# u x D accumulated by TensorE in the turned sums, gate and GLU read from PSUM, seven of 32 products on GpSimd, in a fused selective-scan layer

## The reference

```python
x  = x + attn(rotate_and_decay(x, condB_deltat))      # residual 1
x  = x + ffn(lora_mlp(x, expert_ids))                 # residual 2

def attn(x):
    xn  = layer_norm(x) * ln_g + ln_b
    x_f = mamba(xn)
    x_r = flip(mamba(flip(xn, 1)), 1)
    y   = gelu(concat([x_f, x_r]) @ dim_reduce_w.T + dim_reduce_b)
    g   = y @ glu_w.T + glu_b
    return g[..., :H] * sigmoid(g[..., H:]) + x

def mamba(x):
    xi, z = split(x @ in_proj_w.T)                    # 256 channels each
    u     = silu(causal_conv4(xi) + conv_b)
    dt, B, C = split(u @ x_proj_w.T)                  # 64, 16, 16
    delta = softplus(dt @ dt_proj_w.T + dt_proj_b)
    h_t   = exp(delta_t * A) * h_(t-1) + delta_t * u_t * B_t   # 16 states a channel
    y_t   = sum over the 16 states of h_t * C_t
    return ((y + u * D) * silu(z)) @ out_proj_w.T

def lora_mlp(x, e):   # relu MLP 128 -> 512 -> 128, weights merged with expert e's LoRA
def ffn(x):           # (silu(w1 x) * (w2 x)), gelu(h1 .), gelu(h2 .), w3
```

## Time and profile before

| | before |
|---|---|
| median of 3 runs | 1112.46 us (1112.07 to 1113.34) |
| the profiled execution's own time | 1109.67 us |
| its span, first to last instruction | 1107.5 us |
| mean granted TensorE clock | 0.937 |
| PE busy | 926.2 us, 84% |
| DVE busy | 921.2 us, 83% |
| POOL busy | 874.9 us, 79% |
| ACT busy | 775.3 us, 70% |
| ACT_TABLE_LOAD at L502 | 74 times, 94.9 us |
| scans | 256, the first at 61.65 us, the last at 1011.89 us |

### The profile page before, as it was taken

How to read it: one execution, slowest core, us unless ns; L and a number is a source line. 1 busy time by engine, 2 the same in 40 slices (tenths; PEclk the granted TensorE clock), 3 DMA queues, 4 the chain that set the end, 5 groups by cost and what they waited for, 6 DMA issues and landing times.

```text
span 1107.5 us, 12870 instructions
## 1 busy us (share of the span) xinstructions
PE 926.2 (84%) x4088; PEld 562.7 (51%) x4088; DVE 921.2 (83%) x663; ACT 775.3 (70%) x1139; POOL 874.9 (79%) x399
## 2 busy tenths in 40 slices
PE   2738884799979999899989898989989997698877
PEld 1225562565546555465447544655546545555523
DVE  1088999999899989999899989999999989996110
ACT  4563475759796887778795979688777878465531
POOL 1099898998899898989999889989898898982000
PEclk9858886899999999999999999999989999899998
DMA  5254667453664455454656375545545464632000
GB/s 191 67 174 169 190 216 246 146 186 94 222 186 135 124 199 187 149 155 145 189 150 188 84 231 178 148 124 187 198 150 144 145 210 138 189 105 86 10 1 9
DMA packets 91490, 167.39 MB, mean 151 GB/s; under 512 B 11232, under 2 KB 18720, under 8 KB 91168
## 3 DMA queue, kind: packets, MB, share of 16 engines
q1 hardware_dynamic: 91424, 166.58, 48.5%
HBM read 159.19 MB, written 7.34 MB: 150 GB/s over the span
## 4 chain that ended last, share of the span: by engine, by line
PE 30%; DVE 22%; issue 13%; ACT 11%; POOL 7%; DMA 1%; DVEq 0%; SPq 0%; POOLq 0%; ACTq 0%
DVE bank_d L797 13%; PE bank_m L991 7%; PE bank_y L1076 7%; PE bank_m L997 7%; ACT bank_d L614 4%; POOL state L471 3%; DVE state L795 3%; POOL state L476 2%; PE bank_m L939 2%; ACT L502 2%; PE bank_m L933 2%; PE bank_m L1003 1%; DVE ysum L810 1%; DVE x1T L827 1%; DVE hidB L839 1%
## 5 line engine op out<-in xcount | busy, mean ns | idle before, releaser
L471 POOL TENSOR_TENSOR state<-du,b_rows 128x1024 f32<-128x1024 f32 x256 | 613.1, 2417 | 43.8 <-PE bank_y L1076 42.1
L797 DVE TENSOR_TENSOR_SCAN bank_d<-bank_d,state 128x1024 f32<-128x1024 f32 x184 | 420.7, 2286 | 33.9 <-ACT bank_d L614 30.4
L614 ACT ACTIVATE bank_d<-delta,a_neg 128x512 f32<-128x512 f32 x512 | 330.3, 681 | 103.5 <-DVE state L802 83.4
L1076 PEld LDWEIGHTS bank_y<-ident,state 128*128 128x128 f32 x2048 | 246.8, 148 | 137.3 <-issue 92.8
L1076 PE MATMUL bank_y<-ident,state 128*128 128x128 f32 x2048 | 274.2, 285 | 45.3 <-POOL state L476 25.7
L802 DVE TENSOR_TENSOR state<-bank_d,c_rows 128x1024 f32<-128x1024 f32 x184 | 225.2, 1224 | 7.8 <-DMA c_rows<-bc_store 1.5
L476 POOL TENSOR_TENSOR state<-state,c_rows 128x1024 f32<-128x1024 f32 x72 | 172.7, 2398 | 14.0 <-DVE state L795 14.0
L795 DVE TENSOR_TENSOR_SCAN state<-bank_d,state 128x1024 f32<-128x1024 f32 x72 | 164.1, 2279 | 0.5 <-ACT bank_d L614 0.5
L997 PE MATMUL bank_m<-hidA,h_s 128*128 128x512 f32 x256 | 122.7, 627 | 21.5 <-ACT hidA L665 21.5
L991 PE MATMUL bank_m<-hidB,h_s 128*128 128x512 f32 x256 | 116.9, 602 | 14.1 <-DVE hidB L839 14.1
L921 PE MATMUL bank_m<-xnT,w_conv 128*128 128x512 f32 (+3 forms) x256 | 116.0, 597 | 2.7 <-ACT xnT L548 2.2
(11 more groups left out here) (112 smaller groups left out, 985.4 us busy)
## 6 DMA issues: line engine op xcount, KB each, us to landing
b_rows<-bc_store SPq DMA_DIRECT2D x256, 256.0 KB, 4.6
c_rows<-bc_store SPq DMA_DIRECT2D x256, 256.0 KB, 4.7
wsel<-merged SPq DMA_DIRECT2D x32, 512.0 KB, 5.1
merged<-hidA SPq DMA_DIRECT2D x8, 512.0 KB, 4.0
xin<-in_x SPq DMA_DIRECT2D x8, 256.0 KB, 6.9
h_s<-in_h SPq DMA_DIRECT2D x2, 1024.0 KB, 7.4
out<-tok SPq DMA_DIRECT2D x8, 256.0 KB, 2.4
bc_store<-dbc SPq DMA_DIRECT2D x16, 64.0 KB, 1.6
```

The lines of the kernel that those rows point to most:

```text
L471: nc.gpsimd.tensor_tensor(split(unit_state(u)), du[:, d, :, :width(g)], per_half(b_rows, u), ALU.mult).then_inc(S.bx_ready, 1)
L614: ins = act.activation(split(unit_decay(u))[:, h], delta[:, d, h, :width(g)], ACT.Exp, scale=a_neg[:, h, n:n + 1])
L797: dve.tensor_tensor_scan(decay, decay, drive, 0.0, ALU.mult, ALU.add).then_inc(S.scanned, 1)
L1076: ins = pe.matmul(bank_y[:, h, s * P:(s + 1) * P], split(unit_state(u))[:, h, s * LEN:(s + 1) * LEN], ident[:, :], start=(n == 0 and s == ...
```

## The change

- **u x D.** A tile `skip` holds D on the diagonal of two 128 x 128 matrices. `turn_y` starts each half of bank_y with a matmul of u by this diagonal and accumulates the turning transposes onto it. `take_y` is gone.
- **Gate.** `gate_y` reads bank_y in PSUM and writes `gated`; for d = 1 it writes and reads z backwards.
- **GLU.** ScalarE no longer copies glu0; DVE computes (glu0 + bias) x sigmoid from PSUM in one instruction, then adds the residual as before.
- **Units on GpSimd.** POOL_UNITS has seven places in place of nine.
- **First and last group.** Tables FIRST_GROUP and LAST_GROUP shift places for these two. In group 0 SiLU is applied while u is taken; in group 7 SiLU and GELU are applied while gate, h1 and h2 are taken, and the whole-tile passes are left out there.
- **Order.** Nearly all numbers of the tables are new. The expert weights are loaded by one DMA at each of four places; before, four in a row.
- **Buffers.** `tok` shares a buffer with `cT`.

```diff
-POOL_UNITS = (1, 4, 8, 11, 14, 18, 22, 25, 29)
+POOL_UNITS = (3, 8, 12, 17, 21, 26, 30)
...
-TURN = (19.0, 34.0)
+TURN = (19.0, 36.0)
...
-BY_VECTOR = ("res", "up0", "up1", "up2", "up3", "w3")
+BY_VECTOR = ("glu0", "res", "up0", "up1", "up2", "up3", "w3")
...
+def slot(table, g, name, k=None):
+
+    at = table[name] if k is None else table[name][k]
+    if g == 0:
+        return at + FIRST_GROUP.get(name, 0.0)
+    return at + LAST_GROUP.get(name, 0.0) if g == NG - 1 else at
...
+        def wait_u(eng, g, d):
+            if g == 0:
+                wait_taken(eng, g, *(("uf0", "uf1"), ("ur0", "ur1"))[d])
+            else:
+                eng.wait_ge(S.u_ready, 2 * (g - 1) + d + 1)
+
+        def wait_hidden(eng, g, name):
+
+            if g == NG - 1:
+                wait_taken(eng, g, *all_of(name))
+            else:
+                eng.wait_ge({"gate": S.gate_ready, "h1_": S.h1_ready, "h2_": S.h2_ready}[name], g + 1)
...
-                return act.activation(dst if d == 0 else dst[:, ::-1], bank(g, name), ACT.Identity, bias=c("conv_b", h))
+                if g == 0:
+                    use_table(SILU)
+                return act.activation(dst if d == 0 else dst[:, ::-1], bank(g, name), ACT.Silu if g == 0 else ACT.Identity, bias=c("conv_b", h))
...
-                return act.activation(gate[:, f, :width(g)], bank(g, f"gate{f}"), ACT.Copy, scale=c("w1_s", f))
+                if g == NG - 1:
+                    use_table(SILU)
+                return act.activation(gate[:, f, :width(g)], bank(g, f"gate{f}"), ACT.Silu if g == NG - 1 else ACT.Copy, scale=c("w1_s", f))
...
+            def skip_weights():
+                dve.wait_ge(S.ident_ready, 1)
+                for h in range(HALVES):
+                    ins = dve.tensor_scalar(skip[:, h], ident[:, :], c("skip_d", h), None, ALU.mult)
+                ins.then_inc(S.skip_ready, 1)
...
-            def take_y(g, d):
+            def gate_y(g, d):
                 dve.wait_ge(S.y_turned, 2 * g + d + 1)
-                wait(dve, S.gated_ready, 2 * g + d)
-                w = width(g)
-                for h in range(HALVES):
-                    dst = ysum[:, h, :w] if d == 0 else ysum[:, h, :w][:, ::-1]
-                    ins = dve.scalar_tensor_tensor(dst, (u_f, u_r)[d][:, g % 2, h, :w], c("skip_d", h), bank_y[:, h, :w], ALU.mult, ALU.add)
-                ins.then_inc(S.y_taken, 1)
-
-            def gate_y(g, d):
-                dve.wait_ge(S.y_taken, 2 * g + d + 1)
                 dve.wait_ge(S.z_ready, g + 1)
                 if g > 0:
                     wait_filled(dve, g - 1, "out")
                 w = width(g)
-                dve.tensor_tensor(gated[:, d, :, :w], ysum[:, :, :w], z[:, g % 2, :, :w], ALU.mult).then_inc(S.gated_ready, 1)
+                dst, gate_z = gated[:, d, :, :w], z[:, g % 2, :, :w]
+                if d == 1:
+                    dst, gate_z = dst[:, :, ::-1], gate_z[:, :, ::-1]
+                dve.tensor_tensor(dst, bank_y[:, :, :w], gate_z, ALU.mult).then_inc(S.gated_ready, 1)
...
-                dve.tensor_tensor(x1T[:, :w], glu_a[:, :w], glu_t[:, :w], ALU.mult).then_inc(S.x1_ready, 1)
-                dve.wait_ge(S.x1_ready, g + 1)
+                dve.scalar_tensor_tensor(x1T[:, :w], bank(g, "glu0"), c("glu_b", 0), glu_t[:, :w],
+                                         ALU.add, ALU.mult).then_inc(taken_of(g, "glu0"), 1)
+                wait_taken(dve, g, "glu0")
...
             def turn_y(g, d):
                 pe.wait_ge(S.y_copied, 2 * g + d + 1)
+                wait(pe, S.skip_ready, 1)
+                w = width(g)
                 for h in range(HALVES):
+                    pe.matmul(bank_y[:, h, :w], skip[:, h], (u_f, u_r)[d][:, g % 2, h, :w], start=True, stop=False, skip_group_check=True)
                     for s in range(sequences(g)):
-                        ins = pe.transpose(bank_y[:, h, s * LEN:(s + 1) * LEN], y_rows[:, h, s * P:(s + 1) * P], ident[:, :])
+                        ins = pe.matmul(bank_y[:, h, s * LEN:(s + 1) * LEN], y_rows[:, h, s * P:(s + 1) * P], ident[:, :],
+                                        start=False, stop=True, is_transpose=True, skip_group_check=True)
                 ins.then_inc(S.y_turned, 1)
```

149 lines of the change are left out of this document (76 added, 73 removed), and 16 rows, old and new, of tables (FILL, FIRST_GROUP, LAST_GROUP).

## The result

The changed kernel takes 1102.93 us (median of four, 1101.99 to 1104.27) against 1112.26 us for the kernel before on the same chip: a ratio of 0.9918, 95% interval 0.9900 to 0.9936. It is 9.3 us faster; I had forecast 21. The profiled execution took 1101.99 us with a span of 1100.1.

The account below looks back on a forecast made before the run. It took DVE, busy 113.3 of 120.05 us per group, as the bound, with TensorE only 0.95 us to spare. Scans -8, start -5.6 and tail -6.3 gave -20 us from 1112.46: 1091 predicted, range 1066 to 1108.

Parts of the forecast that it names:

- VectorE's work: DVE's work in a middle group falls by 2.8 us through gate, GLU product and dropped additions, despite two more weighed units.
- ScalarE's two stalls: DVE's stalls on ScalarE's decays before units 0 and 9 are 1.4 and 2.1 us, together 3.5 instead of 4.8.
- DVE therefore waits 47.4 - 43.7 = 3.7 us more for TensorE: Per middle group, DVE waits 3.7 us longer, partly at the GLU product and the rest at the gate.
- my 47.4: TensorE's stretch from gy to the end of the turn: the earlier 43.5 us plus 3.9 of new work.
- rival 1: TensorE hides all its added work; a group falls by 5 us instead of 1, time 1068, chance 0.25.
- so a middle group ... six times: -6: Each middle group goes from 120.05 to 119 us, -1, counted for six groups as -6.
- I forecast +1.4 for it: Group 0 gains only 0.6 us, but group 1's normalising statistics move behind its unit 0 for +2.
- I had 38.6: Before the first scan, TensorE's last convolution ends at about 38.6 and dbc follows at full speed; the stretch gains 5.6 us.
- bank wait of 0.75: Before the first scan, a wait of TensorE for a bank, 0.75 us, goes away.
- Out, which I had 5.5 later: In the tail, out comes 5 us later behind group 6's GELU, plus 1.75 for the skip, less one sum: +5.5.
- the gate: At the tail's gate the whole-tile pass goes and the table load stays: -2.6 us.
- rival 3: The groups gain nothing and one of the ends fails too: 1101 to 1110 us, chance 0.12.

Follow-up runs that it names:

- Experiment 7: Each skip matmul issued twice, so the result has u x 2D, against experiment 2's kernel; 1117.6 us.
- experiment 11: Skip matmuls left out and eight filler passes put on TensorE ahead of its wait for gy, against experiment 2's kernel; 1089.7 us.
- Experiment 2: FIRST_GROUP's entries for group 0's back end taken out of the changed kernel; 1090.94 us.
- experiment 6: FIRST_GROUP's entries h2_0 to h2_3, w3, tok and store taken out of the changed kernel; 1103.4 us.
- experiment 9: FIRST_GROUP's gate, up and h1 entries put back into experiment 2's kernel; 1095.7 us.
- experiment 10: FIRST_GROUP's entries from out to wo put back into experiment 2's kernel; 1090.8 us.
- experiment 5: FIRST_GROUP's entry "gated" taken out of the changed kernel, so group 0's two gates stand 1.5 units later; 1102.1 us.
- experiment 8: Group 6's first GELU moved ahead of the last unit's decays, with one table load more, against experiment 2's kernel; 1088.37 us.
- experiment 12: LAST_GROUP's front-end entries taken out of experiment 8's kernel; 1088.4 us.
- experiment 3: The two skip matmuls per group left out of the changed kernel, so u x D is missing; 1113.0 us.

## Why the prediction was half right

**Middle groups.** VectorE's work (-2.83, forecast -2.8) and ScalarE's two stalls (1.60 and 2.12, forecast 1.4 and 2.1) were right. The term "DVE therefore waits 47.4 - 43.7 = 3.7 us more for TensorE" was mis-sized: it measured 0.87 + 0.73 = 1.6. Experiment 7 shows that more work on TensorE costs its full price, so rival 1 (TensorE hides all) is wrong; experiment 11 shows that the skip matmuls themselves cost 0.3 us per group. The Trainium skill's page "Perfetto Trace Analysis", section "Identifying the Most-Contended Engine", would have judged TensorE by its weight loads (and by its share of peak FLOPs, which I did not work out). The weight loads are busy 67.27 of 118.38 us, 57%, which promises room for more work; experiment 7 found none, so by that measurement they are no sign of slack here. The mechanism was right and its size was not: the stretch from gy to the turn was 2.0 us shorter than my 47.4. Most of that is the clock. I had added the new work to the 43.5 us of the kernel before, and these contained passes at half speed behind the wait of 4.33 us: glu1's two took 1.79, and the eight behind them 1.91, where eight take 1.04 at full speed:

```profile
572.62 1.91 PE L1076 MATMUL bank_y<-ident,state 128*128 128x128 f32 x8
```

The granted clock was 0.71 in these 6 us. After the change the wait is 2.34, the clock stays at 1.00, and glu1 takes 1.10: 1.6 us of the 2.0. Groups 3 and 5 so gained 3.1 to 3.3 us, and group 4, with its h1 product at half speed, 1.7; the mean is 1.7 more than forecast.

**Groups 1 and 2: the step that failed.** I wrote "so a middle group ... six times: -6" and took groups 1 and 2 for middle groups. Their back end is group 0's, and FIRST_GROUP moves it: I read that table for the front end only. Experiment 2 takes those entries out, and groups 1 and 2 fall to 118.2 and 118.4, within 1 us of the 119 of the forecast; these places cost 4.4 and 3.1 us, which the prediction put at nothing. Experiments 6, 9 and 10 name the parts: gate, up and h1 (6.9 alone, 2.0 of it up to unit 24 with the gate takes ahead of the decays, 4.9 after the late up takes), w3 taken two units early (3.1), out to wo (about 1). They don't add up: relieve one stall and, in part, the next grows (experiment 5), and the clock falls at other places.

**Group 0.** I forecast +1.4 for it and it was +5.3. The gate that stands 1.5 units early is 3.5 to 4.5 of it (experiments 2 and 5), so this too was FIRST_GROUP's back end; without it the group is at 121.5, 0.5 over the forecast. Unchanged instructions, though, differ by 2.8 us there between profiles: in the short ones (118.7) the granted clock is 0.97 in the window from 92.5 to 97.5 us, in the others it is 0.50 there, and VectorE waits 2.6 to 2.8 us for a merge. Sixteen passes of the sums of states there take 1.97 us in experiment 8 and 3.67 in experiment 2, whose instructions are the same up to that point. What makes the clock rise earlier in some is open, and no experiment here changed it alone; that it is the cause is argued, not shown.

**Groups 6 and 7.** Group 7's -4 was right. For group 6 I had -1 and it was +2.1: LAST_GROUP's front-end places, which act in it, are at least 1.6 of the 3.1 between them (experiment 12), the same oversight as in group 1. Experiment 12's group 6 has the 5.40 us of h1 that cost group 4 its 1.4, the changed kernel's has 3.70 there; so these places may be all of the 3.1, which is not tested apart. Group 6 was also 2.2 shorter than its neighbours already before, and I took a middle group's gain from it.

**Before the first scan.** The mechanism held; dbc starts at 40.27 where I had 38.6. The four passes of z take 3.55 us, and I had them at full speed. In the kernel before, convolutions stood in that place and began at half speed too, but only the first four passes (21.91 to 25.33); after the change it is the first seven, z's and three of the convolutions (22.05 to 27.98). These three cost about 1.2 us. Another 0.5 is a slip of mine: the "bank wait of 0.75" that I let go is not there, since TensorE was busy 17.35 of the 17.36 us from 21.90 on. Why the slow start lasts longer stays open.

**Tail.** h1 to h2 fell by 3.26 (forecast 3.2), h2 to w3 by 4.5 and w3 to the end by 1.2 (forecast 1.9 + 4.1 together): right, 5.8 for 6.0. Wrong were three others. Out, which I had 5.5 later, came 7.2 later: the first h2 product of group 6, ahead of it, found TensorE idle for 3.55 us and ran at half speed for a time, 5.37 for 3.67, which experiment 8 takes away. The residual's product must wait until glu0's bank is free, so the addition comes 0.8 later. And the gate gained 1.7 of 2.6: the table load now stands between the first gate product and its take (1052.97 to 1054.26 in the chain). Together 3.4 of the 3.7 that are missing.

So 9.3 us instead of 21: 3.9 lost in group 0, 6.0 in groups 1 and 2, 3.1 in group 6, 3.7 in the tail, 1.4 before the scans, against 5.0 won in groups 3 to 5; 13.1 net, which is the profile's -7.4 for -20.5 (the medians differ by 9.3). The time is rival 3's (1101 to 1110), but by another way: the middle groups did gain, and the groups beside them lost it.

## What to carry to other kernels

A table of exceptions for the first or last round of a pipeline acts in the rounds in which that work runs, not in the round it is named after: cost it there, entry by entry. Behind a short ring of buffers, a take that waits for another engine should not stand ahead of the instruction that refills the ring: it cost 2.0 us here. And a take that frees a bank for TensorE should not come late: one unit later, with the clock that fell behind it, went with 4.9 us, more than the change saved in a group. Work taken off an engine can make it slower: look at what stands behind its longest wait before removing what fills the time.

## What the hardware showed

- TensorE idle for 4.07 us before a matmul of 512 columns had it at 2.05 us in place of 1.10, and the granted clock of the 7.5 us behind at 0.56; after 2.34 us idle it stayed at 1.00. In the kernel before, 4.33 us idle went with 1.79 for the same product. Sixteen passes of 256 columns in the gap kept it at full speed (experiments 3 and 11). The effect, 2.3 us per group, is larger than the work removed gave back.
- The length of a wait does not tell it alone. In groups 3, 4 and 5 TensorE waits 1.13 us before dbc and 1.33 before dt, just ahead of the first h1 product; in group 4 the granted clock then is 0.68 and the eight passes take 5.40 us, in the other two 1.00 and 3.70. The group with 5.40 is 1.4 us longer.
- Group 7 took 111.8 us in some kernels and 114.4 to 115.1 in others with the same instructions (experiments 5, 6, 10); where it was long, VectorE waited 2.15 to 3.15 us for the turned y in place of 0.59, and in experiment 10 the granted clock of the group's first 10 us was 0.83 in place of 1.00. Group 1 of experiment 6 is 3.1 us longer than the changed kernel's in the same way. A kernel's time carries such differences of 2 to 3 us that the edit does not explain, so a single group's length is to be read together with its clock.
- z's four passes, TensorE's first long work, took 3.55 us, half speed, while the window from 22 to 26 us has a granted clock of 1.00. The three passes behind them were as slow, and so were the first four of the kernel before. There the column does not explain the duration.
